# Value and gate part vg1 between near2 and near3, an own tile for the transposed input, the output projection in two halves

## The reference, cut to what matters

```python
x = x + attn(x); x = layernorm(x); x = x + ffn(x); x = layernorm(x)    # x: 16 batches x 512 tokens x 256
# attn: 16 heads of 16; keys only at 39 offsets: 0..32, 48, 64, 96, 128, 192, 256, 384
scores = stack([einsum('bhnd,bhnd->bhn', q, shift(k, delta)) for delta in OFFSETS]) * scale + pos_bias
alpha  = softmax(scores); flat = sum(alpha[..., i] * shift(v, OFFSETS[i]))
out    = flat * sigmoid(x @ Wgate + bgate) @ Wout + bout
# ffn: a router (two layers) picks 2 of 8 experts for each token, at most 1024 tokens for an expert
```

## Time and profile before

| | before |
|---|---|
| median of 3 runs | 1766.84 us (1765.27 to 1768.31) |
| profiled execution | 1772.04 us, span 1770.3 us |
| PE busy | 1355.1 us (77%), 31,232 matmuls |
| DVE / ACT / POOL busy | 968.0 (55%) / 902.0 (51%) / 711.6 us (40%) |
| mean granted TensorE clock | 0.793 |

### The profile page before, as it was taken

The page is one execution under the profiler, slowest core; times in us unless marked ns, Lnnn a source line. Parts: engine busy times, 40 slices in busy tenths (PEclk is TensorE's granted clock), DMA queues, the critical chain, the costliest instruction groups (busy, mean ns, idle before and its releaser), DMA issues. The chain is left out here.

```text
span 1770.3 us, 69102 instructions
## 1 busy us (share of the span) xinstructions
PE 1355.1 (77%) x31232; PEld 867.7 (49%) x31232; DVE 968.0 (55%) x2079; ACT 902.0 (51%) x1551; POOL 711.6 (40%) x653
## 2 busy tenths in 40 slices
PE   3556687786978888787787969787753999999960
PEld 1334354444545454555455545454432666666640
DVE  3225456564656755566565746656553555555426
ACT  4134364453746546464544636454543655555517
POOL 5123144353636445364443626344332133333346
PEclk9567696777868778787777869676766999999985
DMA  7655263533426353453634425252322344444239
GB/s 198 167 143 126 84 150 86 128 95 106 118 76 162 89 126 90 100 126 89 151 71 112 96 83 140 67 137 54 103 37 86 84 96 96 96 96 96 37 36 380
DMA packets 194694, 195.49 MB, mean 110 GB/s; under 512 B 61711, under 2 KB 178527, under 8 KB 191152
## 3 DMA queue, kind: packets, MB, share of 16 engines
q1 hardware_dynamic: 176208, 167.44, 35.9%
q0 software_dynamic: 15360, 15.10, 5.5%
q10 hardware_dynamic: 2832, 8.52, 1.2%
HBM read 115.63 MB, written 86.25 MB: 114 GB/s over the span
## 5 line engine op out<-in xcount | busy, mean ns | idle before, releaser
L415 POOL TENSOR_TENSOR p<-p 128x512 f16<-128x512 f32 x96 | 130.2, 1356 | 262.7 <-ACT p L832 262.6
L860 ACT COPY featT<-gp 128x1024 f16<-128x1024 f16 x96 | 93.0, 1023 | 270.3 <-PE gp L577 270.3
L1169 POOL DMA_INDIRECT disp<-y,sidx x128 | 187.8, 1467 | 55.7 <-issue 37.8
L1441 POOL DMA_INDIRECT xln<-y,place x64 | 103.4, 1615 | 222.3 <-DVE y L1581 203.7
L584 PE MATMUL gp<-featT,wr 128*128 128x512 f16 x768 | 186.0, 398 | 5.2 <-issue 2.9
L415 DVE TENSOR_TENSOR p<-p 128x512 f16<-128x512 f32 x96 | 83.0, 865 | 194.0 <-ACT p L832 193.9
L831 ACT ACTIVATE p<-st 128x512 f16<-128x512 f32 x192 | 116.8, 609 | 79.1 <-PE st L629 45.5
L1538 ACT ACTIVATE h<-up,v_near 128x512 f16<-128x512 f32 x128 | 88.2, 689 | 130.8 <-issue 124.0
L1156 POOL TENSOR_TENSOR x<-xin,x 128x1024 f16<-128x1024 f32 x16 | 34.0, 2127 | 276.1 <-ACT x L867 276.1
L1591 DVE TENSOR_TENSOR h<-h 128x512 f16<-128x512 f32 x128 | 88.7, 694 | 72.8 <-ACT h L1539 72.8
L629 PE MATMUL st<-qs,ks 49*64 49x32 f16 (+1 forms) x4096 | 102.2, 197 | 33.0 <-issue 32.9
(11 more groups left out here) (191 smaller groups left out, 3046.1 us busy)
## 6 DMA issues: line engine op xcount, KB each, us to landing
v_near<-v_dram SPq DMA_DIRECT2D x32, 528.0 KB, 7.8
qk_dram<-qk SPq DMA_DIRECT2D x64, 256.0 KB, 3.6
o_dram<-o_far SPq DMA_DIRECT2D x64, 136.0 KB
o_back<-o_dram SPq DMA_DIRECT2D x16, 544.0 KB, 4.2
v_dram<-vs SPq DMA_DIRECT2D x16, 528.0 KB, 3.2
v_far<-v_dram SPq DMA_DIRECT2D x64, 132.0 KB
disp<-y ACTq DMA_DIRECT2D x8, 1040.0 KB, 7.1
rows<-disp SPq DMA_DIRECT2D x16, 520.0 KB, 3.6
```

The lines of the kernel that those rows point to most:

```text
L415: engine.tensor_tensor(p16[:, b, 1, :], p32[:, b, :], p16[:, b, 0, :], ALU.subtract).then_inc(is_split, 1)
L860: gp_done(nc.scalar.copy(featT[:, i, :, :].rearrange("f c t -> f (c t)"), bank[:, :].bitcast(F16)), n, stage, PART_OF_T[stage], i)
L1169: nc.gpsimd.indirect_dma_start(out=disp[:, :], out_offset=bass.IndirectOffsetOnAxis(ap=sidx[:, t, k:k + 1], axis=0), in_=y16[n.par][:, t, ...
L1441: nc.gpsimd.indirect_dma_start(out=xln[:, :], out_offset=bass.IndirectOffsetOnAxis(ap=place[:, gr, t:t + 1], axis=0), in_=y[:, gr, t, :], ...
```

## The change

vg1 moves from slot 3 to slot 8, between near2 and near3. The output projection becomes w0 and w1, one bank each, with near0 between them, and its statistics a part of their own, s. Scores k = 3 go from slot 7 to 8; the split of k = 3 from 9 to 10, its values from 10 to 9; the copies out of the far groups and the first near merge change slot (3, 5, 8 to 2, 4, 9). Since vg1 now reads the transposed input when the tile would hold other rows, the input gets a tile of its own, xT; the output projection and the router share rowT. Waits for the use of featT become x_used and row_used.

```diff
-    3: [("rank", "l"), ("proj", "vg1")], 4: [("outp", "t")], 5: [("rank", "c")],
-    6: [("outp", "w"), ("maxp", "near0")],
-    7: [("outp", "y"), ("maxp", "near1")], 8: [("maxp", "near2"), ("maxp", "near3")],
+    3: [("rank", "l")], 4: [("outp", "t")], 5: [("rank", "c")],
+    6: [("outp", "w0"), ("maxp", "near0"), ("outp", "w1"), ("outp", "s")],
+    7: [("outp", "y"), ("maxp", "near1")], 8: [("maxp", "near2"), ("proj", "vg1"), ("maxp", "near3")],
...
-         ("outp", "t"): 2, ("outp", "w"): 2, ("maxp", "near0"): 2, ("maxp", "near1"): 2, ("maxp", "near2"): 2,
+         ("outp", "t"): 2, ("outp", "w0"): 1, ("outp", "w1"): 1, ("maxp", "near0"): 2, ("maxp", "near1"): 2, ("maxp", "near2"): 2,
...
-SCORES_AT = [-1, 0, 5, 7, 10, 12]
+SCORES_AT = [-1, 0, 5, 8, 10, 12]
 EXP_AT = [[-1, 1, 5, 8, 11, 13], [0, 1, 5, 8, 11, 13]]
-SPLIT_AT = [1, 2, 6, 9, 12, 14]
-VALUES_AT = [2, 4, 7, 10, 13, 16]
-EVAC_AT = [3, 5, 8, 11, 14, 16]
+SPLIT_AT = [1, 2, 6, 10, 12, 14]
+VALUES_AT = [2, 4, 7, 9, 13, 16]
+EVAC_AT = [2, 4, 9, 11, 14, 16]
...
-        featT = sb("featT", [P, 2, CT, N], F16)
+        xT = sb("xT", [P, 2, CT, N], F16)
+        rowT = sb("rowT", [P, 2, CT, N], F16)
...
+        def x_used(eng, n):
+
+            if n.c >= 1:
                 full(eng, n.shift(-1), "proj", "vg1", 1)
+
+        def row_used(eng, n):
+
+            if n.c >= 1:
+                full(eng, n.shift(-1), "rout", "h3", 1)
...
-                elif part == "w":
-                    drained(pe, n, "outp", "t", 0)
-                    drained(pe, n, "outp", "t", 1)
-                    for u in range(2):
-                        bank, is_full = unit(n, "outp", "w", u)
+                elif part[0] == "w":
+                    if part == "w0":
+                        drained(pe, n, "outp", "t", 0)
+                        drained(pe, n, "outp", "t", 1)
+                    for u in (int(part[1]),):
+                        bank, is_full = unit(n, "outp", part, 0)
...
-                if part == "w":
-                    wait(dve, y_stored, n.at(16))
-                    wait(dve, yh_ready, n.at(1))
+                if part[0] == "w":
+                    if part == "w0":
+                        wait(dve, y_stored, n.at(16))
+                        wait(dve, yh_ready, n.at(1))
+                        dve.wait_ge(xres_ready, n.at(1, 1))
+                    u = int(part[1])
+                    bank = full(dve, n, "outp", part, 0)
+                    gp_done(nc.vector.scalar_tensor_tensor(y32[:, 2 * u:2 * u + 2, :], bank[:, :].rearrange("q (t d) -> q t d", t=2), 1.0 / WS,
+                                                           xres[:, 2 * u:2 * u + 2, :], ALU.mult, ALU.add), n, "outp", part, 0)
+                elif part == "s":
                     for u in range(2):
-                        bank = full(dve, n, "outp", "w", u)
-                        dve.wait_ge(xres_ready, n.at(1, 1))
-                        gp_done(nc.vector.scalar_tensor_tensor(y32[:, 2 * u:2 * u + 2, :], bank[:, :].rearrange("q (t d) -> q t d", t=2), 1.0 / WS,
-                                                               xres[:, 2 * u:2 * u + 2, :], ALU.mult, ALU.add), n, "outp", "w", u)
-                    for u in range(2):
-                        drained(dve, n, "outp", "w", u)
+                        drained(dve, n, "outp", f"w{u}", 0)
                     for t in range(TILES):
                         nc.vector.bn_stats(stats[:, t, :], y32[:, t, :]).then_inc(ln_step, 1)
...
-                elif part == "w":
+                elif part == "s":
                     pool.wait_ge(var_ready, n.at(TILES, TILES))
```

More of the change, by code:

```diff
@@ L471, in head @@
                     if n.i is not None or n.c > 0:
-                        drained(sp, n.shift(-1), "outp", "w", 1)
+                        drained(sp, n.shift(-1), "outp", "w1", 0)
                     sync.dma_start(xres[:, :, :], g["x_rows"][bass.ds(n.at(N), N), :].rearrange("(t p) d -> p t d", p=P)).then_inc(xres_loaded, 16)
@@ L692, in proj @@
                         bank, is_full = unit(n, "proj", part, t % 2)
-                        last = terms(lambda a, c: featT[:, a, c, P * t:P * (t + 1)], lambda b, c: wvg[:, b, c, :], bank[:, :])
+                        last = terms(lambda a, c: xT[:, a, c, P * t:P * (t + 1)], lambda b, c: wvg[:, b, c, :], bank[:, :])
                         last.then_inc(is_full, 1)
@@ L759, in outp @@
                     transposes(n, "outp", "t", 1, lambda t, c: og16[:, 1, t, P * c:P * (c + 1)])
-                elif part == "w":
-                    drained(pe, n, "outp", "t", 0)
-                    drained(pe, n, "outp", "t", 1)
-                    for u in range(2):
-                        bank, is_full = unit(n, "outp", "w", u)
+                elif part[0] == "w":
[4 more added lines that the diff above has]
+                        bank, is_full = unit(n, "outp", part, 0)
                         for t in (2 * u, 2 * u + 1):
-                            last = terms(lambda a, c: featT[:, a, c, P * t:P * (t + 1)], lambda b, c: wout[:, b, c, :],
+                            last = terms(lambda a, c: rowT[:, a, c, P * t:P * (t + 1)], lambda b, c: wout[:, b, c, :],
                                          bank[:, D * (t % 2):D * (t % 2 + 1)])
@@ L852, in tail, with transposed @@
                         clear_slots(nc.scalar, disp, y16[0], c).then_inc(cleared, 16)
-            def transposed(n, stage, used):
+            def transposed(n, stage, dst, used):
                 for i in range(2):
@@ L859, in transposed @@
                         used()
-                    gp_done(nc.scalar.copy(featT[:, i, :, :].rearrange("f c t -> f (c t)"), bank[:, :].bitcast(F16)), n, stage, PART_OF_T[stage], i)
+                    gp_done(nc.scalar.copy(dst[:, i, :, :].rearrange("f c t -> f (c t)"), bank[:, :].bitcast(F16)), n, stage, PART_OF_T[stage], i)
             PART_OF_T = {"feat": "x", "outp": "t", "rout": "t"}
@@ L869, in feat @@
             def feat(n, part):
-                transposed(n, "feat", lambda: feat_used_before_proj(act, n))
+                transposed(n, "feat", xT, lambda: x_used(act, n))
             def proj(n, part):
@@ L903, in outp @@
                 if part == "t":
-                    transposed(n, "outp", lambda: feat_used_by_proj(act, n))
+                    transposed(n, "outp", rowT, lambda: row_used(act, n))
                 elif part == "y":
@@ L917, in rout @@
                 if part == "t":
-                    transposed(n, "rout", lambda: full(act, n, "outp", "w", 1))
+                    transposed(n, "rout", rowT, lambda: full(act, n, "outp", "w1", 0))
                 else:
```

4 lines of the change are left out of this document (2 added, 2 removed).

## The result

The changed kernel takes **1784.98 us** (median of 5 runs, 1776.99 to 1786.72) against 1766.84 for the kernel before (1762.07 to 1768.31): ratio 1.0081, 95% interval 1.0052 to 1.0110. It is slower; forecast was 1746. The profiled execution took 1786.72 us, span 1785.0, against 1772.04 and 1770.3 before.

What follows compares the result with a forecast made beforehand. Bound by VectorE's wait for o_back, with everything after its landing on the path. Store -0.5, after landing -0.4, clock -0.6: -1.5 us a pass, -21 over 14 passes, from 1766.84 to 1746 us; range 1712 to 1786.

Steps and rivals of the forecast that it cites:

- What bounds: TensorE idles until o_back lands; work moved ahead of the landing is worth 0, the 19.8 us to the router product count.
- if TensorE is late before the landing: Stated sign of being wrong: TensorE's early part, ahead of o_back's landing, would then have been no spare time.
- Earlier copy: Far evacuation two places earlier on ACT lets o_far's store go sooner; bounds 0 and 2.8 us, taken -0.5 a pass.
- After the landing: From o_back's landing to scores 4: 10.5 to 11.9 us against 11.6 before; middle, -0.4 us a pass.
- the wait: New TensorE wait at group 3's values behind near3, for VectorE's reductions and split of their weights; 2.2 us.
- The page gaps: TensorE waiting for code between landing and scores 4: 2.1 us before, taken 0.5 after, as the new wait hides them.
- The clock: TensorE's half clock falls later or rises earlier with vg1 at the landing; bounds -2.0 and 0, taken -0.6 us.
- First and last passes: Said only to differ from the 14 full passes that carry the change; no time was given for them.
- Rival C: Slower: the new wait at group 3's values costs more than the near steps replaced; +1.4 us a pass, 1787 us; chance 0.26.

Runs made afterwards that it cites:

- e8: Changed kernel with SyncE issuing o_far's store and o_back's load ahead of the low halves of q and k; 1770.28 us, ratio 1.0049 to the kernel before.
- e10: Changed kernel with vg1 back in slot 3, group 3's values behind far0, and SyncE issuing o_far's store and o_back's load before the low halves; 1754.48 us.
- e3: Changed kernel with both vg1 back in slot 3 and the values of group 3 back behind far0; 1759.27 us, ratio 0.9940 to the kernel before.
- e1: Changed kernel with only vg1 put back in slot 3; 1759.13 us, ratio 0.9944 to the kernel before.
- e2: Changed kernel with only the values of group 3 put back behind far0 (slot 10); 1763.22 us, ratio 0.9977 to the kernel before.
- e9: Kernel before with only scores 3, the split of group 3 and the first near merge one slot later; 1752.01 us, ratio 0.9924.
- e7: Kernel before with SyncE issuing o_far's store and o_back's load ahead of the low halves of q and k; 1789.98 us, ratio 1.0148.
- e12: Kernel before with later scores 3, split 3 and first merge, early o_far copies, and SyncE's o_far store and o_back load before the low halves; 1767.40 us.
- e13: Changed kernel with the split of group 3 one slot earlier (9 for 10), ahead of the first near merge; 1771.73 us, ratio 1.0033 to the kernel before.

## Why the prediction was wrong, step by step

A middle pass was to get 1.5 us shorter (-0.5 - 0.4 - 0.6) and got 0.5 us longer (-0.1 + 0.9 - 0.3).

- **What bounds.** "TensorE has spare time before o_back lands" held for the kernel before, not for the changed one. I priced everything that was taken from or put into the stretch ahead of the landing at 0, vg1's departure and the halves alike. But vg1's first half was to be done ahead of the landing, its second half to wait for near2's first reduction. In 10 of 15 passes TensorE was not early enough to wait, and in the pass shown the whole of vg1 lies behind the landing. The 0 for vg1's departure was wrong too: with it gone the clock fell earlier, and the time at half clock ahead of the landing rose from 5.85 to 9.64 us. This is what I had named as a reason to be wrong ("if TensorE is late before the landing").
- **Earlier copy.** Taken -0.5 us a pass, measured -0.1 at the landing; the lower bound, 0, was right. With the DMA engines busy the landing did not move, and e8 and e10 show that even 6 to 8 us would have been worth little.
- **After the landing**, the step that failed. Taken 10.5 to 11.9 against 11.6 us, so -0.4; measured 12.0 against 11.1 in the mean of the middle passes, +0.9. The chain was right, its sizes were not. Up to near3 it took 4.45 us (sum: 1.8 and 1.38 to 2.76, so 3.2 to 4.6): vg1's half ran at half clock, where I took the middle between half and full. near3 and the wait took 3.7 (1.28 and 2.2), since the split took 1.1 to 1.4 us instead of 0.69; values 0.75 (1.0); far0 3.1 (2.4 and 0.5 for pages). That is the sum at its half-clock end, 11.9. And the 11.6 that I compared it with was one pass; the mean of the kernel before is 11.1. The pass shown, 13.2 us (737.09 to 750.28), is one of the longest, with 1.42 of page gap in far0 alone.
- **The page gaps.** I let the wait give back 1.6 us of them up to scores 4 (2.1 to 0.5); 0.9 came back (1.70 to 0.84 in the mean). I did not see that vg1 takes the same idle time: it covered 2.5 us of what e3 had left, the wait then found 1.1. Each move alone pays for itself in e1 and e2.
- **The clock.** Taken -0.6, measured -0.3 from scores 4 to the router product. It did rise behind vg1, as said, and the half-clock part of the stretch is 2.8 us shorter; vg1 itself ran at the low clock, and the half-clock time ahead of the landing grew by 3.8 us; both cost what that gives.
- **First and last passes.** Not priced; in these two traces they cost +4.0 and +4.5 us, more than half of the whole. One execution against another is a weak measure of it: behind the last projections e3, which is faster than the kernel before, takes 8 us longer than it (623.0 against 614.9). 1.8 us of the end are seen: where no near0 stands between the halves, w1 waits for the residual of w0 (the wait of L583 for L1037, twice 0.9). The rest stays open.
- **Rival C** was the case that came: the wait that it names, of the values behind near3, is there, and so is its condition, half clock through vg1 and fewer gaps given back (0.9) than the difference of 1.9 that this makes. But its sum, +1.4 a pass, was too much for the middle passes (+0.48), and the first and last, which it doesn't name, made up for it: that its 1787 lies near the 1785 measured is in part luck.
- **The gain I missed.** near1's reductions ahead of the merge, which the sum used only as a premise, are worth 0.8% with scores 3 and its split moved along, and nothing else (e9). The change contains them and spends more than that.

## What to carry to other kernels

Idle time can be filled once: before two moves are each credited with hiding the same gaps, list the gaps and who takes which. Where an engine waits for a transfer, check that everything which is taken out ahead of it, at the clock that it will then have, leaves it waiting; an experiment that makes the transfer earlier, with an eye on what it puts later (e7, e12), tells whether it bounds. And where a change is a bundle, the cheapest part (three numbers of a table here) may be all of the gain.

## What the runs showed of the hardware

TensorE's longest gaps without a wait stand where the DMA engines are busy: 4.08 us in far0 with a DMA share of 0.56 (e7), 0.55 in the same place in the earlier trace rows. In the middle passes of the kernel before, of 47 such gaps with a DMA share under 0.1 in the 4 us up to their end none was longer than 1.9 us; of 46 with 0.3 or more the longest was 4.8. Many gaps at a high share are short too, and no run shows that the one causes the other. The Trainium skill (Runtime: NRT & Kernel Launch, Instruction fetch mechanics) calls the cost of a code block's boundary mostly hidden; if these gaps are such boundaries, as their distance of 128 matmuls suggests, their 0.55 to 4.08 us do not agree with that.

VectorE's split of group 3 took 0.69 us in all 16 passes of e13, where no GpSimd instruction ran beside it, and 1.1 to 1.4 us in 15 passes of the changed kernel, where GpSimd's split ran beside it. Groups by line, shapes apart (total, mean ns), of the changed kernel and of e13:

```profile
L414 DVE TENSOR_TENSOR p<-p 128x512 f16<-128x512 f32 x96 | 90.8, 946 | 166.9 <-ACT p L832 166.9
```

```profile
L414 DVE TENSOR_TENSOR p<-p 128x512 f16<-128x512 f32 x96 | 81.9, 854 | 220.7 <-ACT p L832 220.7
```

The difference, 8.9 us, is nearly all group 3's, some 0.6 us in each of 15 passes, and lies in the wait for the split. In the pass shown GpSimd's split ended at 745.08 and VectorE's at 745.64, 0.56 later. The Trainium skill (Trainium Architecture — The Big Picture, What this means for kernel authors) says that these two engines share a port by an exclusive lock; that agrees with these rows (0.69 us with GpSimd's split elsewhere, 1.37 with it beside), but no run here tells a lock from another way of sharing.
